# A four-layer graph network: statistics of two tiles in one bn_stats, and the scan of the head scores moved into the node outputs' stage

## What is computed

```
def _layernorm(x, axis=-1, eps=1e-05):
    m = jnp.mean(x, axis=axis, keepdims=True)
    v = jnp.var(x, axis=axis, keepdims=True)
    return (x - m) / jnp.sqrt(v + eps)
...
        e = jax.nn.leaky_relu(alpha_s[src] + alpha_d[dst], negative_slope=0.2)
        m = jax.ops.segment_max(e, dst, num_segments=n_nodes)
        e = jnp.exp(e - m[dst])
        denom = jax.ops.segment_sum(e, dst, num_segments=n_nodes)
        alpha = e / (denom[dst] + 1e-16)
```

## Time and profile before

| | us |
|---|---|
| median of 3 runs (lowest to highest) | 4019.06 (4015.88 to 4021.55) |
| profiled execution | 4020.56 |
| its span | 4018.8 |

### The profile page before, as it was taken

How to read it: one execution, slowest core, us unless ns; L and a number is a source line. 1 busy time by engine, 2 the same in 40 slices (tenths; PEclk the granted TensorE clock), 3 DMA queues, 4 the chain that set the end, 5 groups by cost and what they waited for, 6 DMA issues and landing times. The chain is left out here.

```text
span 4018.8 us, 66244 instructions
## 1 busy us (share of the span) xinstructions
PE 3075.4 (77%) x13334; PEld 1749.4 (44%) x13334; DVE 3290.3 (82%) x9625; ACT 2173.0 (54%) x5748; POOL 2085.5 (52%) x2017
## 2 busy tenths in 40 slices
PE   4866757777749997569995658999979999218886
PEld 1255644444424443124442545555546666104443
DVE  6979979999969997768786877888956666779997
ACT  0048868999952322442221776777746666115554
POOL 5945557766637551037660006666645555006676
PEclk9967778999969998889997888999989999659998
DMA  2069987877742221689993994555545565213332
GB/s 56 3 189 311 308 268 234 253 246 245 246 118 74 69 69 36 183 226 278 282 276 103 287 268 108 143 143 142 137 148 194 197 199 190 68 46 112 114 113 86
DMA packets 635184, 679.72 MB, mean 169 GB/s; under 512 B 168901, under 2 KB 496159, under 8 KB 628581
## 3 DMA queue, kind: packets, MB, share of 16 engines
q1 hardware_dynamic: 587012, 575.17, 45.7%
q0 software_dynamic: 48000, 102.76, 11.6%
HBM read 385.35 MB, written 296.91 MB: 170 GB/s over the span
## 5 line engine op out<-in xcount | busy, mean ns | idle before, releaser
L1411 PE MATMUL r_pM<-r_masked,wr 128*128 128x512 f32 x1600 | 712.8, 596 | 10.7 <-DVE r_masked L1356 10.7
L1356 DVE SCALAR_TENSOR_TENSOR r_masked<-r_typ,r_hT 128x512 f32<-128x512 f32 x800 | 495.4, 690 | 101.7 <-ACT r_hT L1389 78.7
L1411 PEld LDWEIGHTS r_pM<-r_masked,wr 128*128 128x128 f32 x1600 | 295.4, 191 | 357.4 <-issue 291.9
L691 POOL DMA_INDIRECT q_rows<-nr,row_x x200 | 259.2, 1296 | 194.8 <-PE q_pT L600 134.5
L2432 POOL DMA_INDIRECT out<-o_base,o_at_o x200 | 266.1, 1331 | 134.4 <-issue 66.3
L691 POOL DMA_INDIRECT r_xs<-h_tab,r_at_s x200 | 229.9, 1149 | 87.7 <-issue 47.0
L691 POOL DMA_INDIRECT r_xs<-tab,r_at_s x200 | 212.1, 1060 | 87.9 <-issue 46.5
L691 POOL DMA_INDIRECT e_zd<-xz,dst_c x200 | 191.7, 959 | 90.4 <-issue 52.6
L691 POOL DMA_INDIRECT i_hs<-hr,i_at_s x200 | 191.3, 957 | 87.8 <-issue 47.1
L2240 ACT ACTIVATE q_eo<-q_pO,b 128x512 f32<-128x512 f32 x196 | 134.7, 687 | 172.5 <-PE q_pO L2275 148.8
L691 POOL DMA_INDIRECT e_zs<-xz,src_c x200 | 190.4, 952 | 71.0 <-issue 59.1
(11 more groups left out here) (426 smaller groups left out, 9141.8 us busy)
## 6 DMA issues: line engine op xcount, KB each, us to landing
xz<-na_xz SPq DMA_DIRECT2D x49, 1040.0 KB, 5.8
r_typ<-vec_s SPq DMA_DIRECT2D x100, 256.0 KB, 4.5
g_al<-alpha_s SPq DMA_DIRECT2D x100, 256.0 KB, 4.3
na_xz<-in_x SPq DMA_DIRECT2D x49, 512.0 KB, 6.9
tab<-na_x SPq DMA_DIRECT2D x49, 512.0 KB, 2.8
e_xin<-tab SPq DMA_DIRECT2D x49, 512.0 KB
hr<-e_hh SPq DMA_DIRECT2D x49, 512.0 KB, 3.2
nr<-e_n SPq DMA_DIRECT2D x49, 512.0 KB
```

What stands on the lines that cost most here:

```text
L691: pool.indirect_dma_start(dest[:, j, :], None, table, bass.IndirectOffsetOnAxis(ap=index[:, j:j + 1], axis=0), element_offset=first).then_ ...
L1356: v.scalar_tensor_tensor(masked[:, r, :], typ[d.slot(4)][:, :], float(r), hT[d.slot(2)][:, :], ALU.is_equal, ALU.mult).then_inc(ev.mk, 1)
L1411: pe.matmul(pM[s][:, :], g.wr[:, layer * R_ + r, :], masked[:, r, :], start=(r == 0), stop=(r == R_ - 1)).then_inc(ev.mm, 1)
```

## The change

It has two parts. First, `stats` now gives two tiles to one bn_stats, read alternately (one element of the one tile, one of the other), so that the even half of its result is the first tile's mean and sum of squares and the odd half the second's. The aggregates, their wait and `pair_stats` go; the sum of squares is divided by 128 where it is used. Second, the spreading of the 12 destination scores moves into gat_rows, in two halves of 6 heads: one scan at most to a turn of DVE, the ends and carries turned by way of small DRAM buffers instead of PE. SP's and DVE's programs there are written out. The source scores are no longer spread: head_softmax uses each node's own one at the last slot of its segment only, and folds it into the max and sum scans.

The diff, where "..." stands for what is left out (the same edit of the statistics recurs in relations, aggregate_rows and interaction, and what read the mean at place 0 reads it at place 1):

```diff
--- before.py
+++ after.py
@@ -571,27 +571,23 @@
             pe.matmul(p0, g.b1_col[:, 0:1], g.ident[:, :], start=True, stop=True).then_inc(s_pe, 1)
-def stats(v, c, g, x4, st, mv, done):
+def stats(v, x, mv, done):
+    for j in range(0, x.shape[1], 2):
+        last = v.bn_stats(mv[:, j:j + 2, :].rearrange("p t c -> p (t c)"), x[:, j:j + 2, :].rearrange("p t f -> p f t"))
+    last.then_inc(done, 1)
+def rstd(a, g, c, mv, rs, done):
+    c.step(a.activation(rs[:, :], mv[:, :, 2], ACT.Ln, bias=g.eps_ln[:, :], scale=1.0 / P))
+    a.activation(rs[:, :], rs[:, :], ACT.Exp, scale=-0.5).then_inc(done, 1)
+def normalise(v, x4, mv, rs, y4, done):
     for j in range(J):
-        last = v.bn_stats(st[:, j, :], x4[:, j, :])
-    c.step(last)
-    v.sem_inc(g.state.waits, 1)
-    for j in range(J):
-        last = v.bn_aggr(mv[:, j, :], st[:, j, :])
-    last.then_inc(done, 1)
-def rstd(a, g, c, mv, rs, done):
-    c.step(a.activation(rs[:, :], mv[:, :, 1], ACT.Ln, bias=g.eps_ln[:, :]))
-    a.activation(rs[:, :], rs[:, :], ACT.Exp, scale=-0.5).then_inc(done, 1)
-def normalise(v, x4, mv, rs, y4, done):
-    for j in range(J):
-        last = v.tensor_scalar(y4[:, j, :], x4[:, j, :], mv[:, j, 0:1], rs[:, j:j + 1], ALU.subtract, ALU.mult)
+        last = v.tensor_scalar(y4[:, j, :], x4[:, j, :], mv[:, j, 1:2], rs[:, j:j + 1], ALU.subtract, ALU.mult)
     last.then_inc(done, 1)
@@ -871,10 +855,10 @@
...
-                    pair_stats(v, c, g, lambda j: rows[:, j, 0:P], st, mv[s], ev.st)
+                    stats(v, rows[:, :, 0:P], mv[s], ev.st)
...
-                    v.tensor_scalar(ve[s][:, :], mv[s][:, :, 1], EPS_LN, None, ALU.add).then_inc(ev.ve, 1)
+                    v.tensor_scalar(ve[s][:, :], mv[s][:, :, 2], 1.0 / P, EPS_LN, ALU.mult, ALU.add).then_inc(ev.ve, 1)
...
@@ -1091,11 +1075,13 @@
...
-                    pair_stats(v, c, g, lambda j: z_tile(n1, j), stz, mvz, nd.sz)
+                    for j in range(0, 2 * J, 2):
+                        last = v.bn_stats(mvz[:, j:j + 2, :].rearrange("p t c -> p (t c)"), z_tiles(n1, j).rearrange("p (t f) -> p f t", t=2))
+                    last.then_inc(nd.sz, 1)
...
-                    pair_stats(v, c, g, lambda j: hh[n2.slot(4)][:, j, :], sth, mvh, nd.sh)
+                    stats(v, hh[n2.slot(4)], mvh, nd.sh)
...
@@ -2132,13 +2115,21 @@
...
     w_a, l_n = ([g.sem(f"q_{n}{k}") for k in range(2)] for n in ("wa", "ln"))
-    s_0 = g.sem("q_zero")
+    s_0, s_v = g.sem("q_zero"), g.sem("q_v")
+    l_t, d_ends, w_ends, l_rows, d_row, w_row, l_carry, d_sum = (g.sem("q_" + n) for n in ("lt", "de", "we", "lr", "dr", "wc", "lc", "ds"))
+    HALF = NH // 2
+    ENDS, LATE, ROWS, CARRY = (4, 28), (9, 33), (14, 38), (18, 42)
...
         n_, base = some("n", 2, [P, 2 * J, P]), some("base", 4, [P, 2 * J, P])
+        ends, whole, carry = sb("ends", [P, HALF]), sb("whole", [P, 1]), sb("carry", [P, HALF])
+        row_ends, row_whole, row_carry = (sb(n, [HALF, P]) for n in ("rowe", "roww", "rowc"))
+        spread = g.wr[:, :, :].rearrange("p a b -> p (a b)")[:, 0:HALF * W].rearrange("p (k w) -> p k w", w=W)
+        backwards = lambda a: a[:, ::-1]
+        heads_of = lambda h: g.att_s[2 * NH + h * HALF:2 * NH + (h + 1) * HALF, :]
...
         bank = lambda n: ctx.enter_context(nc.psum_tensor("q_" + n, [P, HW], F32))
@@ -2151,7 +2142,34 @@
...
         def _(sp):
+            def scores(t):
+                for h in range(2):
+                    if t == LATE[h] + 1:
+                        sp.wait_ge(d_ends, h + 1)
+                        sp.dma_start(g.ends_s[h], ends[:, :]).then_inc(w_ends, 16)
+                        if h == 0:
+                            sp.dma_start(g.whole_s.unsqueeze(1), whole[:, :]).then_inc(w_ends, 16)
+                    if t == LATE[h] + 2:
+                        sp.wait_ge(w_ends, 32 + 16 * h)
+                        sp.dma_start(row_ends[:, :], g.ends_s[h].rearrange("p k -> k p"), allow_slow_non_contiguous=True).then_inc(l_rows, 16)
+                        if h == 0:
+                            sp.dma_start(row_whole[:, :], g.whole_s.partition_broadcast(HALF)).then_inc(l_rows, 16)
+                    if t == ROWS[h] + 1:
+                        sp.wait_ge(d_row, h + 1)
+                        sp.dma_start(g.carry_s[h], row_carry[:, :]).then_inc(w_row, 16)
+                    if t == ROWS[h] + 2:
+                        sp.wait_ge(w_row, 16 * h + 16)
+                        sp.dma_start(carry[:, :], g.carry_s[h].rearrange("k p -> p k"), allow_slow_non_contiguous=True).then_inc(l_carry, 16)
+                if t == CARRY[0] + HALF:
+                    sp.wait_ge(d_sum, 1)
+                    sp.dma_start(spread, wide_rows(heads_of(1))).then_inc(l_t, 16)
+            sp.dma_start(spread, wide_rows(heads_of(0))).then_inc(l_t, 16)
             def turn(pair, edges):
+                b = edges(0)
+                if b:
+                    scores(b.k)
...
                     wait_alone(g, sp, nd.fo, p.now())
@@ -2170,7 +2188,7 @@
...
                     sp.dma_start(g.att_s[0:NH, b.span()], att[b.slot(2)][:, :]).then_inc(w_a[b.slot(2)], 16)
-            braid.sweep(sp, turn)
+            braid.written_out(turn)
...
             for k in range(4):
@@ -2208,8 +2226,40 @@
...
                 v.tensor_tensor(rows, four(pU[m][:, :]), rows, ALU.add).then_inc(nd.fo, 1)
+            c = Chain(v, s_v)
+            def scores(t):
+                for h in range(2):
+                    dest = lambda k: backwards(g.state.scores[:, h * HALF + k, :])
+                    if t == ENDS[h] - 1:
+                        v.wait_ge(l_t, 16 * h + 16)
+                        if h == 0:
+                            v.tensor_reduce(whole[:, :], g.more_w[:, :], AX.X, ALU.min)
+                            v.memset(row_carry[:, :], 0.0)
+                        c.step(v.tensor_tensor(spread, spread, each(g.last_w, HALF), ALU.mult))
+                    if ENDS[h] <= t <= LATE[h]:
+                        k = t - ENDS[h]
+                        scan = v.tensor_tensor_scan(dest(k), backwards(g.more_w[:, :]), backwards(spread[:, k, :]), 0.0, ALU.mult, ALU.add)
+                        if t == LATE[h]:
+                            c.step(scan)
+                            if h:
+                                v.wait_ge(w_ends, 32)
+                            v.tensor_copy(ends[:, :].unsqueeze(2), g.state.scores[:, h * HALF:(h + 1) * HALF, 0:1]).then_inc(d_ends, 1)
+                    if t == ROWS[h]:
+                        v.wait_ge(l_rows, 32 + 16 * h)
+                        if h:
+                            v.wait_ge(w_row, 16)
+                        v.tensor_tensor_scan(backwards(row_carry[:, 0:P - 1]), backwards(row_whole[:, 1:P]), backwards(row_ends[:, 1:P]), 0.0,
+                                             ALU.mult, ALU.add).then_inc(d_row, 1)
+                    if CARRY[h] <= t < CARRY[h] + HALF:
+                        k = t - CARRY[h]
+                        v.wait_ge(l_carry, 16 * h + 16)
+                        scan = v.tensor_tensor_scan(dest(k), backwards(g.more_w[:, :]), backwards(spread[:, k, :]), carry[:, k:k + 1], ALU.mult, ALU.add)
+                        if k == HALF - 1:
+                            scan.then_inc(d_sum, 1)
             def turn(pair, edges):
-                n1, n2 = pair(1), pair(2)
+                n1, n2, b = pair(1), pair(2), edges(0)
...
                     s = n1.slot(4)
@@ -2220,11 +2270,13 @@
...
                     features(n1, 1)
+                if b:
+                    scores(b.k)
...
                     unit(n1, 0)
-            braid.sweep(v, turn)
+            braid.written_out(turn)
...
         def _(a):
@@ -2313,15 +2365,16 @@
...
         sb = lambda n, s: ctx.enter_context(nc.sbuf_tensor("h_" + n, s, F32))
-        a_, b_, c_ = sb("a", [P, 3 * NH, W]), sb("b", [P, 2 * NH, W]), sb("c", [P, NH, W])
+        a_, b_, c_ = sb("a", [P, 3 * NH, W]), sb("b", [P, NH, W]), sb("c", [P, NH, W])
+        notlast = sb("notlast", [P, W])
...
         block = ctx.enter_context(nc.Block())
-        logit, own = part(a_, 0), part(b_, 0)
+        logit, own, scores = part(a_, 0), part(b_, 0), g.state.scores
...
         def _(sp):
-            sp.dma_start(a_[:, NH:, :], wide_rows(g.att_s[NH:, :])).then_inc(s_in, 16)
+            sp.dma_start(own, wide_rows(g.att_s[NH:2 * NH, :])).then_inc(s_in, 16)
...
             sp.dma_start(wide_rows(g.alpha3_s[0:NH, :]), part(a_, 2)).then_inc(s_p, 16)
@@ -2333,25 +2386,25 @@
...
             seg.prepare(v, c)
+            c.step(v.tensor_scalar(notlast[:, :], g.last_w[:, :], -1.0, BIG, ALU.add, ALU.mult))
             v.wait_ge(s_in, 16)
-            c.step(v.tensor_tensor(a_[:, NH:, :], a_[:, NH:, :], each(g.last_w, 2 * NH), ALU.mult))
-            seg.scan(v, c, "sum", 2 * NH, a_[:, NH:, :], back=b_[:, :, :])
+            c.step(v.tensor_tensor(own, own, scores[:, :, :], ALU.add))
+            c.step(v.scalar_tensor_tensor(own, own, 0.2, own, ALU.mult, ALU.max))
```

(22 more changed lines are left out.)

61 lines of the change are left out of this document (25 added, 36 removed).

## The result

The changed kernel takes **3900.1 us** (median of 4 runs, 3895.3 to 3902.8), the kernel before 4017.5 beside it (4 runs): ratio **0.9706** (95% interval 0.9689 to 0.9722). It was found again on one chip of the experiments (e5). On the four others the kernel before runs slower. On one of them the changed kernel itself was run and loses to it, and on two more its close variants do; on the fourth only versions with slowed gathers ran.

The account below looks back on a forecast made before the run. VectorE was busiest at 82%, but DMA, ScalarE or TensorE was also full in single stages. Terms -8 - 34 - 0 - 1 - 1 - 30 + 2 = -72 us, from 4020.6 to 3948 us; range 3905 to 3985.

Parts of the forecast that it names:

- The price of the alternating read: New bn_stats on two alternating tiles: 0.52 us each, from the strided reduction's 1.79 ns an element; bounds 0.33 to 0.71.
- node_rows: Statistics to ve take 2.31 us in place of 2.47, 0.16 gained in each of 49 turns: -8 us.
- no penalty: Rival: alternating read costs 1.04 ns an element, 0.33 us per instruction; node_rows -25, sum -100, 3920 us; chance 0.27.
- layer0_edges: DVE saves 0.8 us a turn of 11.1, of which 0.7 counts over about 49 turns: -34 us.
- GpSimd needs 10.0: layer0_edges: GpSimd's turn of 11.11 us, with its 1.42 wait for DVE less 0.3 usual distance, needs 10.0.
- ACT needs 10.2: layer0_edges: ScalarE idles 0.72 and 0.16 us a turn, so it needs 10.2 us of the 11.1.
- Relations, aggregate_rows, interaction: Layer 0 relation stage 0 (PE busy throughout), aggregate_rows -1 (DMA bound), interaction -1 (drain only).
- the ring: interaction's 9.92 us turn runs through DVE's scan, products, PE, ACT, i_pL; shorter statistics only lengthen the scan's wait: -1.
- head_softmax: Six half-size operations replace the product, scans and carries; max scan starts 16.0 us after input instead of 42.67: -30 us.
- gat_rows: Added scans hide in DVE's 2.13 us idle; a 0.61 MB load ahead of the first q_n costs 1.8: +2 us.
- spread scores hold up gat_rows: Rival: four transposed reads queued ahead of loads each cost PE a 9.5 us turn, 38 us back; 3986 us; chance 0.08.
- Slower than before: Rival: alternating read pays twice, 2.54 ns an element, 0.71 us per instruction; +56 us, 4077 us; chance 0.04.

Follow-up runs that it names:

- e5: The changed kernel itself run again, against the kernel before on the same chip: 3902.7 us, ratio 0.9699.
- e3: Changed kernel plus single timed VectorE operations in edge_columns: 1600-element reduction 3006 ns strided, 1820 neighbouring; bn_stats round eight places 590 ns against 428.
- e9: Changed kernel plus timed VectorE operations in edge_columns, varying places gone round and distance: bn_stats 452 ns at three places, 594 at four.
- e2: Changed kernel with node_rows taking statistics of only four of its eight tiles: stage 287.8 us, as with all statistics; total 4269.3 us.
- e8: Kernel before with only gat_rows, head_softmax and gat taken from the change (heads alone): 3992.8 us, ratio 0.9926 of before.

## Why the prediction was right and wrong

- **The price of the alternating read** is the step that failed. "I take the reduction's 1.79 ns, 0.52 us, since it is the nearest row": measured 0.355. Row and penalty were real; the reduction goes round eight places and the new instruction round two, and the penalty begins at four (e3, e9). I matched the rows by the distance of the stride, which plays almost no part, and overlooked the count of places. The row with the 16 B stride is of another sort again: it never comes back to a line, and e9's copies of that sort do pay (244 against 212 ns). The lower end of my bounds, 0.33, was nearly the value.
- **node_rows**, -8, measured -37. Four at 0.355 against the 2.47 us to ve give 1 us of the turn (6.92 to 5.97). Even "no penalty" gave too little (-25), by a slip of its own: the rise from 309 to 346 GB/s was applied to the one turn of 6.92 that I had read, not to the mean, (580.1 - 258.2) / 48.5 = 6.64 from first to last x1. 6.64 x 309 / 347 = 5.91; the mean after is 287.8 / 48.5 = 5.93. The rival had named DMA as next, at 346 GB/s, and 347 was reached; e2 shows that VectorE is no longer the bound.
- **layer0_edges**, -34, measured -50. VectorE's need is mis-sized by the same price: 10 x (0.52 - 0.355) = 1.65 us a turn. "GpSimd needs 10.0" was exact (turn 10.02); "ACT needs 10.2" was high, it is busy 291.4 of 300 us, 9.7 a turn. GpSimd's floor is the turn itself, ScalarE's lies 0.3 us below it; VectorE no longer sets it (253 of 300 us busy). Which of the two does was not separated by a run.
- **Relations, aggregate_rows, interaction**: 0, -1, -1; measured 0 each. In interaction the scan's wait for i_pL grew from 0.7 to 1.6 us a turn in the mean (34.5 us in 48 waits, 79.1 in 50) and the turn stayed: the ring was read rightly.
- **head_softmax**, -30: measured -30.6 between the landmarks, -29.6 with gat_rows (e8). The 16.0 us to the max scan were 16.03.
- **gat_rows**, +2: measured 0, so the load ahead of the first q_n, priced at 1.8 us, cost nothing that shows. Its turn is 9.48 (q_base at 3099.41 and 3108.89), the added scans cost nothing, and the rival "spread scores hold up gat_rows" is refuted by e8.
- **What was missed in all** is 46 us (118 against 72): 29 of them in node_rows and 16 in layer0_edges, both by the price of the read. The sign was right because the heads' 30 us and the aggregates' work stood on rows that held.
- **"Slower than before"** by a read that pays twice is refuted. The kernel does get slower on another chip, by a mechanism that I had not listed: a faster VectorE took away the rests between GpSimd's gathers, and the longer runs of gathers came with the longer stalls. The rows for it were there (the 1.42 us rest of the earlier trace rows, and my own sentence that GpSimd would be nearly full); what a queue without rests does on another chip no row of this trace could show.

## What to carry to other kernels

Before taking the price of a strided access from another row, count how many separate places it goes round, not how far apart they are: two cost nothing here, three next to nothing (22 ns in 430), four or more 0.3 to 0.6 ns an element. When the bound engine gets faster, read its stage by the floors of the other engines over the mean of the turns, not over one turn. And a helper that used to be held back by the bound (here GpSimd with its gathers) runs without rests afterwards: try the result on several chips before believing a gain, and try a pause of 0.3 us ahead of each gather where one stalls.

## What the runs showed of the hardware

- One bn_stats takes 256 fp32 elements of two alternating tiles in 416 ns (0.355 us apart) from SBUF or PSUM; two of 128 took 0.42 (392 kept VectorE busy for 82.1 us), and their aggregates 0.16 more.
- The cost of many places starts between three and four and is the same at 128, 256 and 512 B between them (590, 594, 594 ns); at 800 B it was 618.
- The two kinds of chip run the same program 4% apart (4017 to 4022 against 4176 to 4191 us for the kernel before), most of it in the one stage with eight gathers a turn beside SyncE's transfers. node_rows agrees: 287.8 and 289.1 us, DMA at 344 to 347 GB/s.
- On the stalling chips, beside gathers 1.25 us apart and after some four of them, SyncE's issues come 2.9 to 5.6 us apart instead of 0.5 to 0.9, and ScalarE stands up to 15 us ahead of an instruction for which only TensorE's signals were due, while VectorE's and ScalarE's own instructions last as long as ever.
- TensorE's granted clock is 0.74 of full speed over 640 to 940 us there, against 0.92 in the trace of after. In the stall shown above, which begins at 749.3 us, it is still at 1.00 (2.4 GHz) until 751.5, then at 0.50 (1.2 GHz) from 753.0 to 768.0, and at 1.00 again from 769.5 on, TensorE having been idle from 747.1 to 764.6. So the stall is there before the clock falls, and the clock did not bring it on.
